# ScalarE makes the biases of the row exponentials, Pool's norm steps go first, W_base is turned by half tiles

## What is computed

```python
mod = (_silu(L0_c) @ L0_wmod).reshape(L0_c.shape[0], 6, 1, -1)
sa, ca, ga, sb, cb, gb = (mod[:, 0], mod[:, 1], mod[:, 2], mod[:, 3], mod[:, 4], mod[:, 5])
h = _layernorm(x, axis=-1) * (1 + ca) + sa
x = x + ga * _L0_attn_ref(h, wq, wk, wv, wo)        # rotary q, k; causal softmax; 32 heads
h = _layernorm(x, axis=-1) * (1 + cb) + sb
x = x + gb * _L0_ffn_ref(h, W_base, b_base, W_gate, W_thr, b_thr, A_w, B_w)
# ffn: x @ W_base.T + b_base, and 8 experts of rank 16 (A_w, B_w), weighted by a thresholded gate
```

## Time and profile before

| | |
|---|---|
| time, median of 3 runs | 1724.31 us (1723.79 to 1727.38) |
| time of the profiled execution | 1725.72 us |
| its span (first to last instruction) | 1723.9 us |
| mean granted PE clock | 0.972 |
| busy: PE, DVE, ACT, POOL | 1611.1, 1015.7, 960.1, 605.5 us |
| starts of pairs u=0, 2, 10, 16, 31 (first m_col of DVE) | 143.94, 209.36, 515.46, 724.32, 1224.57 us |
| first body of the last part | 1292.03 us |

### The profile page before, as it was taken

How to read it: one execution, slowest core, us unless ns; L and a number is a source line. 1 busy time by engine, 2 the same in 40 slices (tenths; PEclk the granted TensorE clock), 3 DMA queues, 4 the chain that set the end, 5 groups by cost and what they waited for, 6 DMA issues and landing times. The chain is left out here.

```text
span 1723.9 us, 29774 instructions
## 1 busy us (share of the span) xinstructions
PE 1611.1 (93%) x9530; PEld 1183.2 (69%) x9530; DVE 1015.7 (59%) x3292; ACT 960.1 (56%) x2296; POOL 605.5 (35%) x475
## 2 busy tenths in 40 slices
PE   5888989999899989999999999997889999999996
PEld 2556766666667757777777777774468888888885
DVE  5627676667667647667567666665355354544533
ACT  2336777867778767787887878777621010111100
POOL 3533243443424324233243243330413433434342
PEclk9999999999999989999999999997699999999998
DMA  9583433435353274323322432322561112121210
GB/s 348 204 255 85 99 100 101 109 93 131 83 147 87 59 225 126 90 68 79 98 72 69 98 82 56 90 63 73 132 197 37 58 52 73 37 74 47 63 57 29
DMA packets 170722, 174.46 MB, mean 101 GB/s; under 512 B 20890, under 2 KB 120522, under 8 KB 170580
## 3 DMA queue, kind: packets, MB, share of 16 engines
q1 hardware_dynamic: 168468, 168.54, 35.2%
q10 hardware_dynamic: 2112, 4.19, 0.7%
HBM read 96.65 MB, written 25.18 MB: 71 GB/s over the span
## 5 line engine op out<-in xcount | busy, mean ns | idle before, releaser
L1466 ACT ACTIVATE rows_sb<-rows_sb,bias_m 128x640 f32<-128x640 f32 (+7 forms) x512 | 396.4, 775 | 222.6 <-DVE bias_m L1751 222.3
L1733 DVE CUSTOM_DVE_ANT_0 rows_sb<-ps_t,mask 128x512 f32<-128x512 f32 (+3 forms) x512 | 295.5, 585 | 156.8 <-PE ps_t L1233 148.6
L1502 ACT ACTIVATE probsT<-ps_s 128x512 f32<-128x512 f32 (+2 forms) x640 | 319.8, 546 | 9.5 <-PE ps_s L1264 7.1
L1233 PE MATMUL ps_t<-stk 96*128 96x512 f32 (+3 forms) x768 | 274.5, 361 | 28.8 <-DVE smax L1733 19.6
L1264 PE MATMUL ps_s<-stk 98*128 98x512 f32 (+3 forms) x768 | 237.4, 389 | 17.4 <-ACT probsT L1502 10.7
L1774 DVE TENSOR_TENSOR ps_s<-ps_s,mask_t 128x128 f32<-128x128 f32 (+1 forms) x384 | 120.6, 339 | 156.4 <-PE ps_s L1264 155.0
L1264 PEld LDWEIGHTS ps_s<-stk 98*128 98x128 f32 x768 | 134.4, 196 | 108.4 <-issue 49.3
L1233 PEld LDWEIGHTS ps_t<-stk 96*128 96x128 f32 x768 | 148.3, 193 | 86.3 <-DVE smax L1733 28.2
L1901 POOL TENSOR_TENSOR rope_b<-rope_b,rope_sin 128x512 f32<-128x512 f32 x64 | 82.8, 1293 | 315.9 <-DVE rope_b L1718 315.9
L1291 PE MATMUL ps_pv<-probsT,v_all 128*32 128x256 f32 (+1 forms) x2816 | 187.7, 360 | 1.2 <-ACT probsT L1502 1.2
L1222 PE MATMUL ps_qkv<-hT_hi,w_hi 128*128 128x512 f32 x384 | 159.0, 414 | 6.4 <-DVE hT_lo L1693 2.9
(11 more groups left out here) (199 smaller groups left out, 3042.3 us busy)
## 6 DMA issues: line engine op xcount, KB each, us to landing
stk<-rot SPq DMA_DIRECT2D x384, 128.0 KB, 2.4
...
attn_scratch<-attn_sb SPq DMA_DIRECT2D x128, 64.0 KB, 3.1
...
```

What stands on the lines that cost most here:

```text
L1233: pe.matmul(bank[:, 0:c1 - c0], stk[0:3 * HD, u % 2, 0, qt // 4, h, qt % 4 * P:(qt % 4 + 1) * P], stk[0:3 * HD, u % 2, 1, part, h, 0:c1 - ...
L1466: act.activation(row, row, ACT.Exp, bias=bias_m[:, qt, h:h + 1], scale=SCALE, accum_out=sums[:, qt // 4, h, qt % 4:qt % 4 + 1]).then_inc(s ...
L1502: act.activation(probsT[:, w % 4, hs[0]:hs[-1] + 1, 0:n], s_bank[(NS * u + k) % 3][:, 0:len(hs) * n].rearrange("p (h n) -> p h n", h=len(hs)),
L1733: dve.tensor_tensor_reduce(rows_sb[:, to, at + c0:at + c1], bank[:, 0:n], mask[:, BANK - n:BANK] if last else mask[:, 0:1].broadcast_to([P ...
```

## The change

Six things change.

1. The biases. row_biases (12 instructions a pair on DVE, 384 in all) is gone. In row_exp ACT first waits for the maximum, makes the bias with act.mul, and then waits for its own result.
2. The norm steps in pairs u=2 to 10. ln_norm moves from slot 2 to slot 3; on POOL ln_rstd and next_rest stand ahead of rope_total; on ACT next_round stands first in its slot behind next_out.
3. The start. The matmuls of the first chains are spread over the rows of pair 0 in another way (BEHIND), and rope_products(1, 0) stands behind row 20, not behind all 24.
4. W_base by half tiles. The 22 halves are loaded one by one into eight half buffers. The first halves of W_base's eight tiles come first: they are turned by PE in slots 1 to 8 of the last pair and rounded and rested by DVE one slot later. In the transition 14 are left: six, three and five. SP issues the loads 8 to 15 in pair 31 behind load_wo(7), and the last six behind the first x tile.
5. wo_raw lies in x_next and in the joined h_pair, no longer in w_raw, so load_wo(0) and (1) wait for nothing in pair u=29.
6. At u=13 SP issues load_next_hT(0) behind the six stk and the two m_rows DMAs of the next pair, not ahead of them.

The diff, cut to its core:

```diff
-NORM_STEPS = {1: "stats", 2: "norm", 6: ("turn", 0), 7: ("scale", 0), 8: ("split", 0), 10: ("turn", 1), 11: ("scale", 1),
+NORM_STEPS = {1: "stats", 3: "norm", 6: ("turn", 0), 7: ("scale", 0), 8: ("split", 0), 10: ("turn", 1), 11: ("scale", 1),
               12: ("split", 1)}
...
-BEHIND = [5] * EARLY_ROWS + [3] * (NR - EARLY_ROWS)
+BEHIND = [5] * EARLY_ROWS + [2] * 8 + [4] * 8
...
-        wo_raw = [w_flat[:, i * D:(i + 1) * D] for i in range(2)]
+        wo_raw = [x_next[:, :], h_pair[:, :, :].rearrange("p a n -> p (a n)")]
...
-        stage = [gb[:, 0, :], gb[:, 1, :], bias[:, :], spare[:, :]]
+        stage = [x[:, a * BANK:(a + 1) * BANK] for x in (gb[:, 0, :], gb[:, 1, :], bias[:, :], spare[:, :]) for a in range(2)]
...
-        items = [("ag", 0), ("ag", 1), ("bt", 0)] + [("wb", o) for o in range(KT)]
+        UNITS_ = [("wb", o, 0) for o in range(KT)] + [(kind, k, half) for kind, k in (("ag", 0), ("ag", 1), ("bt", 0))
+                                                      for half in range(2)] + [("wb", o, 1) for o in range(KT)]
+        UNITS, SOON = len(UNITS_), KT
...
-        parts = [slice(0, 4), slice(4, 6), slice(6, len(items))]
+        parts = [slice(SOON, SOON + 6), slice(SOON + 6, SOON + 9), slice(SOON + 9, UNITS)] + [
+            slice(n, n + 1) for n in range(SOON)]
...
-            load_pieces(range(len(stage), len(items)))
+            for n in range(2 * len(stage), UNITS):
+                load_piece(sp, n)
...
+        def rest_weights(dve, part):
+            for n, kind, k, half, bank in turned(part):
...
+                if n < SOON:
+                    dve.wait_ge(st_t, n + 1)
+                    dve.tensor_copy(hi, turns).then_inc(st_hi, 1)
+                dve.wait_ge(st_hi, n + 1)
+                dve.tensor_tensor(lo, turns, hi.bitcast(F32), ALU.subtract).then_inc(st_lo, 1)
...
-                if u == 2 * G - 3:
-                    load_next_hT(0)
                 if u + 1 < PAIRS:
                     sp.wait_ge(st_ok, NS * u)
                     stack(u + 1, 1)
                 place_m(u, 1)
+                if u == 2 * G - 3:
+                    load_next_hT(0)
...
                 if u == PAIRS - 1:
                     load_wo(6)
                     load_wo(7)
+                    for n in range(len(stage), 2 * len(stage)):
+                        load_piece(sp, n)
...
+                    if u == PAIRS - 1 and 0 < i <= SOON:
+                        turn_weights(pe, 2 + i)
...
+                if qt >= 4 or not h:
+                    both = w if qt >= 4 else w + 1
+                    hs = slice(h, h + 1) if qt >= 4 else slice(0, 2)
+                    act.wait_ge(max_ok, NR * u + ENDS[both] + 1)
+                    act.mul(bias_m[:, qt, hs], smax[:, u % 2, qt // 4, hs, qt % 4], -SCALE).then_inc(bias_ok, 1)
                 act.wait_ge(bias_ok, NB * u + bias_no(w) + 1)
...
+                    if step and step[1][0] == "split":
+                        next_round(step[0], step[1][1])
                     if (u, i) in V_AT:
                         copy_v(*V_AT[u, i])
                     row_exps(u + 1, i)
...
                 for k in range(FIRST_ROW[i], FIRST_ROW[i] + ROW_SLOTS[i]) if i in ROW_SLOTS else ():
...
-            rope_products(1, 0)
+                    if k == FIRST_ROPE:
+                        rope_products(1, 0)
...
-                    row_biases(u + 1, i)
+                    if u == PAIRS - 1 and 1 < i <= SOON + 1:
+                        rest_weights(dve, 1 + i)
...
-                    if (u, i) in ROPE_AT:
-                        rope_total(*ROPE_AT[u, i])
                     step = norm_step(u, i)
                     if step and step[1] == "stats":
                         ln_rstd(1, step[0])
                     if step and step[1][0] == "split":
                         next_rest(step[0], step[1][1])
+                    if (u, i) in ROPE_AT:
+                        rope_total(*ROPE_AT[u, i])
```

More of the change, by code:

```diff
@@ L614, in phase_b_sync, with turn_weights @@
             sp.wait_ge(out_st, 16 * B * NT)
+        def turn_weights(pe, part):
+            for n, kind, k, half, bank in turned(part):
+                if n == SOON:
+                    pe.wait_ge(max_ok, NR * PAIRS)
+                    pe.wait_ge(m_ok, 2 * PAIRS)
+                    pe.wait_ge(at_ok, 2 * PAIRS)
+                elif n == 0:
+                    pe.wait_ge(vT_ok, 2 * T)
+                pe.wait_ge(st_ld[n % len(stage)], loaded[n])
+                if SOON <= n < SOON + len(turn_bank):
+                    pe.wait_ge(st_lo, SOON)
+                elif n >= 2:
+                    pe.wait_ge(st_lo, n - 1 if n < SOON else n - len(turn_bank) + 1)
+                rows = piece_cols(kind, k)
+                for j in range(4):
+                    mm = pe.transpose(bank[:, j * rows:(j + 1) * rows], stage[n % len(stage)][0:rows, j * P:(j + 1) * P],
+                                      ident[0:rows, 0:rows])
+                mm.then_inc(st_t, 1)
@@ new lines, in rest_weights @@
+        def rest_weights(dve, part):
+            for n, kind, k, half, bank in turned(part):
+                rows = piece_cols(kind, k)
+                hi, lo = piece(kind, k, half)
+                turns = bank[:, 0:4 * rows].rearrange("p (k n) -> p k n", k=4)
+                if n < SOON:
[3 more added lines that the diff above has]
+                dve.tensor_tensor(lo, turns, hi.bitcast(F32), ALU.subtract).then_inc(st_lo, 1)
@@ L616, in phase_b_tensor @@
         def phase_b_tensor(pe):
             pe.wait_ge(at_ok, 2 * PAIRS)
-            def turn_weights(part):
-                for n, i, kind, k, half, bank in turned(part):
-                    if n == 0:
-                        pe.wait_ge(max_ok, NR * PAIRS)
-                        pe.wait_ge(m_ok, 2 * PAIRS)
-                        pe.wait_ge(vT_ok, 2 * T)
-                    if half == 0:
-                        pe.wait_ge(st_ld[i % len(stage)], loaded[i])
-                    if n >= len(turn_bank):
-                        pe.wait_ge(st_lo, n - len(turn_bank) + 1)
-                    rows = piece_cols(kind, k)
-                    for j in range(4):
-                        kt = 4 * half + j
-                        mm = pe.transpose(bank[:, j * rows:(j + 1) * rows], stage[i % len(stage)][0:rows, kt * P:(kt + 1) * P], ident[0:rows, 0:rows])
-                    mm.then_inc(st_t, 1)
@@ L849, in body @@
                     dve.tensor_tensor(x1[:, e, cols], x1[:, e, cols], xn[:, cols], ALU.add).then_inc(last_ok, 1)
-            def rest_weights(part):
-                for n, i, kind, k, half, bank in turned(part):
-                    rows = piece_cols(kind, k)
-                    hi, lo = piece(kind, k, half)
-                    dve.wait_ge(st_hi, n + 1)
-                    dve.tensor_tensor(lo, bank[:, 0:4 * rows].rearrange("p (k n) -> p k n", k=4),
-                                      hi.bitcast(F32), ALU.subtract).then_inc(st_lo, 1)
             dve.wait_ge(wo_lo_ok, KT)
-            rest_weights(0)
+            rest_weights(dve, 0)
             dve.wait_ge(rows_ld, 16 * (B + 1))
@@ L966, in store_next @@
                 sp.wait_ge(ln_lo, NT + 2 * tt + half + 1)
-                for a, part in enumerate((h_next_hi[:, :].bitcast(F32), h_next[:, :])):
+                for a, part in enumerate((h_next_hi, h_next)):
                     sp.dma_start(h_dram[a].rearrange("(k p) t -> p k t", p=P)[
@@ L1405, in next_out @@
                     act.wait_ge(h_st, 32 * (2 * tt + half))
[L1406 removed]
+                act.copy(h_next, bank).then_inc(h_cp[half], 1)
             def next_round(tt, half):
                 act.wait_ge(h_mod[half], tt + 1)
[L1410 removed]
+                act.copy(h_next_hi.bitcast(F32R), h_next).then_inc(ln_hi, 1)
             def split_qk(t, n):
```

92 lines of the change are left out of this document (31 added, 61 removed).

## The result

| | before | after |
|---|---|---|
| time, median | 1724.05 us (4 runs, 1723.79 to 1727.38) | 1676.91 us (4 runs, 1675.78 to 1680.86) |
| span of the profiled execution | 1723.9 us | 1679.1 us |
| PE, DVE, ACT, POOL busy | 1611.1, 1015.7, 960.1, 605.5 us | 1591.7, 965.4, 1038.7, 606.3 us |

The account below looks back on a forecast made before the run. It took PE, busy 65.97 of 66.50 us in two ordinary pairs, as the bound there. Its terms summed to -27.4 us from the profiled 1725.7, giving 1698.3; the median being 1.4 lower, 1697 us, range 1683 to 1715.

Parts of the forecast that it names:

- Even norm pairs: Pairs u=2 to 8: PE gaps of 1.00, 1.95, 0.66, 0.83 and 0.1 of 1.01 go, saving 17.4 us (8 to 22).
- Biases on ACT: Late biases on ACT delay the copy of v in odd pairs by 0.35 us, 12 times: costs 4 us (-3 to +10).
- The price of a bias on ACT: A bias on ACT takes 0.21 us like the logarithms, 0.24 with the wait for its own result.
- Odd norm pairs: Half of the 1.04 us without PE goes in each of four pairs: saves 2 us (0 to 4).
- Clock: PE's clock, 0.96 in u=8, recovers with denser work: saves 1 us (0 to 3).
- Start: PE's gaps of 1.27 and 1.43 us at the end of pair 0's rows shrink: saves 2.5 us (0 to 4).
- u=13: PE's wait mostly moves from the m_rows DMA to hT: saves 1 us (-5 to +2 on the time).
- Last pair: Eight W_base turns take 3.6 to 7 us of PE against 4.89 idle: costs 1 us (-1 to +5).
- Transition: The 5.55 us W_base DMA leaves the chain, eight turns fewer: saves 7.5 us (3 to 10).
- three conditions: Forecast wrong if ordinary pairs take over 34 us, a bias on ACT over 0.3, or the last pair over 27.
- ACT as the bound: Rival: a bias on ACT costs 0.55 us or more, so ACT becomes the bound: 1744 us, chance 0.07.
- The case of "more": Rival: all of the norm pairs' gaps, the clock and 5 us at u=13 go: 1685 us, chance 0.1.

Follow-up runs that it names:

- e2: Changed kernel, with DVE also making the same 384 biases into a tile nobody reads, while ACT uses its own: 1692.49 us, ratio 0.9807.
- e5: The kernel before with the biases on ACT and nothing else changed: 1711.08 us, ratio 0.9910.
- e6: The kernel before with the new order of the norm steps and nothing else changed: 1714.92 us, ratio 0.9928.
- e1: Changed kernel with the biases back on DVE, behind the triangle of their slot as before: 1709.88 us, ratio 0.9897.
- e10: Changed kernel with load_next_hT(0) of pair 13 ahead of the stk DMAs again: 1679.73 us, ratio 0.9732.
- e11: Changed kernel with the 14 W_base turns of the transition as six, two and six, not six, three and five: 1680.32 us, ratio 0.9737.

## Why the prediction was wrong, point by point

- **Even norm pairs: right, with some luck in the size.** 17.4 us taken, 18.2 measured, and the gaps that went are those named: 1.00, 1.95, 0.66 and 0.83, while the 1.01 stayed as 1.17. But the 18.2 hold the clock of u=6 and u=8, some 3.3 us by estimate, so the gaps gave about 15. The reading of the 1.14 us bias as DVE held by POOL is borne out by e2. What the prediction did not see is that these gains hold only together: e5 and e6 add up to 15 us less than both.
- **Biases on ACT: the step that failed.** The term is -4 where +12.2 was measured, 16.2 of the 17.4 us between the sum of 27.4 and the 44.8 of the two spans. It failed twice. It took no credit for DVE in ordinary pairs: "nothing is to be won on DVE" rested on PE's busy 65.97 of 66.50 us, although showed biases of up to 1.155 us, and 0.58 us a pair were won there (e1). And it priced the instruction and not its place: it wrote that where ACT already waited, the maximum comes 0.15 us before DVE's bias, but the bias stood behind a triangle, and in the very row that was quoted ACT now runs 1.41 us earlier. With that, "0.1 + 0.24 + 0.24 = 0.6 us late" at the copy of v is 0.05 us early, and the charge of 4 us has no ground.
- **The price of a bias on ACT: right.** 0.21 us was taken from the logarithms, 0.203 is the median (range 0.185 to 0.235). Its 0.24 with the wait was an upper bound.
- **Odd norm pairs: mis-sized.** 0.5 us each was taken, 1.73 measured, of which e1 gives 1.10 to the biases. The 1.04 us without PE was taken as the whole reserve, again from busy time; PE's busy time itself fell from 34.64 to 33.32 us.
- **Clock: right in direction, too small.** u=8 went from 0.96 to 1.00, but so did u=6, which the prediction did not list; together they are 3.3 us where 1 was taken.
- **Start: 1.8 us up to u=2 for 2.5 taken.** Not told apart from scatter: u=2 began between 204.4 and 211.6 us in these runs, u=0 between 140.3 and 144.4, with the old and the new start.
- **u=13: right in mechanism**, and worth nothing (e10).
- **Last pair: right in size, for a reason that was wrong.** The turns cost nothing, 23.47 against 23.70 us; but they were priced at half clock, and the clock was 0.93, not 0.64.
- **Transition: 5.2 for 7.5 us**, inside the range, and held back by what its lower end named, the halves loaded behind x. e11 took that wait away and won nothing, so the wait for POOL's a_lo stood right behind it.
- **Signs that failed:** two ordinary pairs take 65.37 us, not 66.5 to 67; PE's wait for the copy of v is 0.34 us each, not 0.7 to 0.9; the wait for hT is 6.84 us, not 3 to 6; the first body comes 38.60 us behind the last pair, not 35 to 38. None of the three conditions under which it called itself wrong came about: it had watched for ordinary pairs that get longer, and they got shorter.
- **Rivals.** ACT as the bound did not come: ordinary pairs have ACT at 58.63 of 65.37 us. The case of "more" was given 0.1 at 1685 us and was itself too small, since it held no gain in ordinary pairs.

One correction: the prediction says of the earlier trace rows that PE waits 12 times, 4.2 us together. The row printed there is one of those waits, of 0.34 us; the sum is this row of the waits before:

```profile
PEld ps_t L1233 <- ACT v_all L1454: 4.2, 12, 0.5
```
